# Head attention beside the main attention: 36 blocks one by one in place of 32 by twos, and experts that add into the output

## The reference, cut to what matters

```python
xn = layernorm(x)                                # x: 4 x 2048 x 256, float32
x  = x + attn(xn) + ffn(xn)

# attn: per token, the 16 heads attend to one another
Q, K, V = (xn @ W + b for each).reshape(B, S, 16, 16); rope on Q, K
out = softmax(einsum('bsid,bsjd->bsij', Q, K) / 4) @ V

# ffn: causal latent attention over the sequence, then 8 experts
x2 = xn + mla(rmsnorm(xn, g1))
t  = rmsnorm(x2, g2); top 2 of 8 by t @ gate_w, softmax of the two
ffn = x2 + sum over the two of gate * (silu(t @ w1[e]) @ w2[e])
```

## Time and profile before

| | us |
|---|---|
| median of 3 runs | 2903.67 (2902.66 to 2905.32) |
| the profiled execution | 2890.86 |
| its span, first to last instruction | 2889.0 |
| projections, to the attention's first POOL instruction | 424 |
| attention | 1546 |
| routing | 256 |
| experts | 633 |
| copy to `out` | 30 |

### The profile page before, as it was taken

The page is one execution under the profiler, slowest core; times in us unless marked ns, Lnnn a source line. Parts: engine busy times, 40 slices in busy tenths (PEclk is TensorE's granted clock), DMA queues, the critical chain, the costliest instruction groups (busy, mean ns, idle before and its releaser), DMA issues. The chain is left out here.

```text
span 2889.0 us, 58374 instructions
## 1 busy us (share of the span) xinstructions
PE 2543.6 (88%) x21356; PEld 1302.9 (45%) x21356; DVE 2236.6 (77%) x3720; ACT 1606.6 (56%) x2421; POOL 2113.7 (73%) x1196
## 2 busy tenths in 40 slices
PE   7999878999999999999999999996673988988892
PEld 4544432333333333333333333224563877777782
DVE  5557858899889988998899989902563899889970
ACT  2322225677777777777777777684442544444441
POOL 4543339698889888988898889884675777778772
PEclk9999999999999999999999999997775999999996
DMA  5785552133233323332333232105865565566555
GB/s 179 228 251 196 170 183 60 49 80 93 53 85 87 93 53 85 87 93 53 84 87 93 54 85 77 44 19 161 263 213 172 116 126 124 122 127 131 126 91 145
DMA packets 235945, 334.91 MB, mean 116 GB/s; under 512 B 30024, under 2 KB 175272, under 8 KB 234920
## 3 DMA queue, kind: packets, MB, share of 16 engines
q1 hardware_dynamic: 208072, 287.54, 34.4%
q0 software_dynamic: 27360, 39.73, 8.0%
q10 hardware_dynamic: 256, 4.19, 0.4%
HBM read 246.96 MB, written 154.04 MB: 139 GB/s over the span
## 5 line engine op out<-in xcount | busy, mean ns | idle before, releaser
L1047 DVE TENSOR_REDUCE p_piece_max<-p_ring 128x1 f32<-128x512 f32 (+3 forms) x2160 | 1293.2, 654 | 136.8 <-PE p_ring L157 66.8
L1105 ACT ACTIVATE p_probs<-p_st 128x1024 f32<-128x1024 f32 (+3 forms) x1280 | 1078.8, 897 | 413.9 <-PE p_st L1168 215.7
L1168 PE MATMUL p_st<-unit_q,unit_k 64*128 64x512 bf16 (+3 forms) x3520 | 432.7, 348 | 39.5 <-ACT p_probs L1105 23.2
L1186 PE MATMUL p_pv<-p_probs,unit_vg 128*32 128x512 f32 (+3 forms) x3520 | 412.1, 543 | 0.0
L1855 POOL DMA_INDIRECT acc<-p_y,p_rows x142 | 223.3, 1573 | 142.7 <-issue 56.1
L170 PE MATMUL p_ring<-unit_k,unit_q 64*128 64x512 bf16 (+3 forms) x1600 | 271.4, 352 | 27.9 <-DVE p_piece_max L1047 25.4
L964 POOL TENSOR_TENSOR p_terms<-p_head_in 128x4096 f32<-128x4096 f32 x32 | 282.9, 8839 | 8.9 <-DMA p_head_in<-head_qkv 4.6
L985 POOL TENSOR_TENSOR p_terms<-p_head_p,p_head_in 128x4096 f32<-128x4096 f32 x32 | 283.3, 8853 | 3.6 <-ACT p_head_p L1112 3.6
L2020 PE MATMUL p_y_ps<-p_w,p_hid 128*128 128x256 f32 x1136 | 276.8, 400 | 0.0
L969 POOL TENSOR_TENSOR p_terms<-p_terms 128x2048 f32<-128x2048 f32 (+2 forms) x96 | 252.7, 2632 | 17.4 <-POOL p_terms L969 11.4
L991 POOL TENSOR_TENSOR p_terms<-p_terms 128x2048 f32<-128x2048 f32 (+2 forms) x96 | 252.6, 2631 | 17.1 <-POOL p_terms L991 11.4
(11 more groups left out here) (192 smaller groups left out, 3477.5 us busy)
## 6 DMA issues: line engine op xcount, KB each, us to landing
p_w<-ffn_w SPq DMA_DIRECT2D x142, 512.0 KB
qk_parts<-p_parts SPq DMA_DIRECT2D x64, 384.0 KB, 3.6
head_qkv<-p_heads SPq DMA_DIRECT2D x16, 1536.0 KB, 6.8
p_rows<-rows_by_expert SPq DMA_DIRECT2D x71, 258.0 KB, 3.5
unit_q<-qk_parts SPq DMA_DIRECT2D x132, 128.0 KB, 3.2
unit_k<-qk_parts SPq DMA_DIRECT2D x132, 128.0 KB, 3.6
v_padded<-p_vx SPq DMA_DIRECT2D x16, 1024.0 KB, 8.0
p_head_in<-head_qkv SPq DMA_DIRECT2D x32, 384.0 KB, 4.2
```

Of the source, the lines that this page charges most:

```text
L1047: nc.vector.tensor_reduce(piece_max[:, n % 2, h:h + heads, i, pc], ring_ps[g % RING][:, 0:heads * width].rearrange("p (h k) -> p h k", h=h ...
L1105: nc.scalar.activation(probs[:, 2 * turn_of(s, i) + u, :, 0:width], st_ps[u][:, :, 0:width], ACT.Exp).then_inc(probs_done, 1)
L1168: last = nc.tensor.matmul(st_ps[u][:, half, 0:width], k6[s][rows, PAIR * second + u, kt * P:(kt + 1) * P], q6[s][rows, PAIR * second + u, ...
L1186: last = nc.tensor.matmul(pv_ps[hh * VW:(hh + 1) * VW, skip:CT], vg[s][:, kt, hh * VW:(hh + 1) * VW], probs[:, 2 * turn_of(s, i) + hh % PA ...
```

## The change

Three things are done. First, the attention stage takes 36 head blocks, the experts' stage 28. The blocks of the attention stage no longer go by twos within a unit but one by one: block m is weighed at about step 18 + 17.3 m of the 640 steps, whatever unit that is in. POOL runs weigh, shift of the next, score of the one after it. The exponentials' sums come first in weighing, and DVE inverts them (`reciprocal`) in place of POOL's `pow`. Three input slots replace two, POOL's loop is written out, and its waits no longer also increment the semaphore `apart`. Second, the routing stores `res` straight into `out`, the experts' stage adds to `out`, blank rows are dropped by a bounds check in the indirect DMA, and the last stage copies nothing. Third, blocks are added by fours with one DMA over two stretches of DRAM, 512 KB: the four early blocks at tile 1, the others at tiles 15, 24, 34, 43, 52, 61 and 70 (`ADDED`).

```diff
+MORE_BLOCKS = 4
+P2_BLOCKS = HEAD_BLOCKS + MORE_BLOCKS
...
+def early_block(m):
+    return block_of(m, 0) if m < HEAD_BLOCKS else block_of(m - MORE_BLOCKS, 1)
...
-        head_in = sb("p2_head_in", [P, 2, 3, H, DH])
+        head_in = sb("p2_head_in", [P, 3, 3, H, DH])
...
-        HEADS_AT = (12, 14)
         INVERSE_AT = 10
-        HEADS_STORED_AT = (12, 20)
+        weighed_at = lambda m: 18 + 173 * m // 10
+        MAXIMA_AT = {11 if m == 0 else weighed_at(m) - 14: m for m in range(P2_BLOCKS + 1)}
+        PROBS_AT = {weighed_at(m) - (1 if m == 0 else 4): m for m in range(P2_BLOCKS)}
+        HEADS_STORED_AT = {weighed_at(m) + 10: m for m in range(P2_BLOCKS)}
...
+        DIVIDED_AFTER = {max(m for m in range(P2_BLOCKS) if weighed_at(m) < N_STEP * (n + 2) - 8): n for n in range(UNITS - 1)}
...
-            def load_heads(m, u):
-                wait_apart(sp, head_done, m + 1, apart)
-                sp.dma_start(head_in[:, u, :, :, :].rearrange("p i h d -> p (i h d)"), head_qkv[block_of(m, 0)]).then_inc(head_loaded[u], 16)
-
-            def store_heads(m, u):
-                wait_apart(sp, head_done, 2 + m + 1, apart)
-                sp.dma_start(attn_rows[block_of(m, 0)], head_o[:, u, :, :].rearrange("p h d -> p (h d)")).then_inc(head_stored[u], 16)
+            def load_heads(m):
+                if m >= 3:
+                    sp.wait_ge(head_done, 2 + m - 2)
+                sp.dma_start(head_in[:, m % 3, :, :, :].rearrange("p i h d -> p (i h d)"), head_qkv[early_block(m)]
+                             ).then_inc(head_loaded[m % 3], 16)
+
+            def store_heads(m):
+                sp.wait_ge(head_done, 2 + m + 1)
+                sp.dma_start(attn_rows[early_block(m)], head_o[:, m % 2, :, :].rearrange("p h d -> p (h d)")
+                             ).then_inc(head_stored[m % 2], 16)
...
-                    if i in HEADS_STORED_AT:
-                        u = HEADS_STORED_AT.index(i)
-                        store_heads(2 * n + u, u)
-                        if n + 1 < UNITS:
-                            load_heads(2 * n + 2 + u, u)
+                    if N_STEP * n + i in HEADS_STORED_AT:
+                        m = HEADS_STORED_AT[N_STEP * n + i]
+                        store_heads(m)
+                        if m + 3 < P2_BLOCKS:
+                            load_heads(m + 3)
...
+            def weigh_heads(m):
+                u = m % 2
+                pool.wait_ge(head_probs_done, m + 1)
+                if m:
+                    pool.wait_ge(head_inverted, m)
+                src = head_p[:, u, :, :]
+                for width in (8, 4, 2):
+                    step(nc.gpsimd.tensor_tensor(head_sum[:, :, 0:width], src[:, :, 0:width], src[:, :, width:2 * width], ALU.add))
+                    src = head_sum[:, :, :]
+                nc.gpsimd.tensor_tensor(head_sum[:, :, 0:1], src[:, :, 0:1], src[:, :, 1:2], ALU.add).then_inc(head_summed, 1)
                 step(nc.gpsimd.tensor_tensor(
                     terms[:, :, :, :], head_p[:, u, :, :].unsqueeze(2).to_broadcast([P, H, DH, H]),
+                    head_in[:, m % 3, 2, :, :].unsqueeze(1).to_broadcast([P, H, DH, H]), ALU.mult))
+                for width in (8, 4, 2):
                     step(nc.gpsimd.tensor_tensor(terms[:, :, :, 0:width], terms[:, :, :, 0:width],
+                                                 terms[:, :, :, width:2 * width], ALU.add))
+                if m >= 2:
+                    pool.wait_ge(head_stored[u], 16 * (m // 2))
+                step(nc.gpsimd.tensor_tensor(head_o[:, u, :, :], terms[:, :, :, 0], terms[:, :, :, 1], ALU.add))
+                pool.wait_ge(head_inverted, m + 1)
...
-                step(nc.gpsimd.tensor_tensor(head_inv[:, :], head_sum[:, :, 0], minus_one[:, :], ALU.pow), before + 9)
...
-            def body(n):
-                for u in range(2):
-                    shift_heads(2 * n + u, u)
-                for u in range(2):
-                    weigh_heads(2 * n + u, u, n, steps(2 * n + 2, 2 * n + u))
-                for u in range(2):
-                    score_heads(2 * n + 2 + u, u, n + 2, steps(2 * n + 2 + u, 2 * n + 2))
-
-            body(0)
-            with pool.Fori(1, UNITS - 1) as n:
-                body(n)
-                divide(n - 1)
-            for u in range(2):
-                shift_heads(2 * (UNITS - 1) + u, u)
-            for u in range(2):
-                weigh_heads(2 * (UNITS - 1) + u, u, UNITS - 1, steps(2 * UNITS, 2 * (UNITS - 1) + u))
-            divide(UNITS - 2)
+            for m in range(2):
+                score_heads(m)
+            shift_heads(0)
+            for m in range(P2_BLOCKS):
+                weigh_heads(m)
+                if m + 1 < P2_BLOCKS:
+                    shift_heads(m + 1)
+                if m + 2 < P2_BLOCKS:
+                    score_heads(m + 2)
+                if m in DIVIDED_AFTER:
+                    divide(DIVIDED_AFTER[m])
...
-            def head_maxima(m, u):
-
-                dve.wait_ge(head_scored, m + 1)
-                nc.vector.tensor_reduce(head_max[:, u, :], head_s[:, u, :, :], AX_X, ALU.max).then_inc(head_max_done, 1)
+            def head_maxima(m):
+
+                if m < P2_BLOCKS:
+                    dve.wait_ge(head_scored, m + 1)
+                    nc.vector.tensor_reduce(head_max[:, m % 2, :], head_s[:, m % 2, :, :], AX_X, ALU.max).then_inc(head_max_done, 1)
+                if m:
+                    dve.wait_ge(head_summed, m)
+                    if m >= 2:
+                        dve.wait_ge(head_done, 2 + m - 1)
+                    nc.vector.reciprocal(head_inv[:, :], head_sum[:, :, 0]).then_inc(head_inverted, 1)
...
-                    if i - 2 in HEADS_AT:
-                        u = HEADS_AT.index(i - 2)
-                        head_probs(2 * n + u, u)
+                    if N_STEP * n + i in PROBS_AT:
+                        head_probs(PROBS_AT[N_STEP * n + i])
...
-                sp.dma_start(acc_v[b, c], res[:, c % 2, :, :]).then_inc(res_stored[c % 2], 16)
+                sp.dma_start(out_v[b, c], res[:, c % 2, :, :]).then_inc(res_stored[c % 2], 16)
...
-            sp.dma_start(acc[T:, :].rearrange("(r p) d -> p r d", p=P), blank[:, :, 0:D]).then_inc(tail_stored, 16)
...
-    NB = T // P - HEAD_BLOCKS
+    NB = T // P - P2_BLOCKS
...
-    sorted_rows, acc, table_i = SHARED["sorted"], SHARED["acc"], SHARED["table"]
+    sorted_rows, table_i = SHARED["sorted"], SHARED["table"]
+    acc = out_v.rearrange("b c p t d -> (b c t p) d")
...
-    ADDED = {STARTS[2 * k + 4] + 2: k for k in range(NB // 2)}
+    ADDED = {STARTS[4 * k + 6] + 2: k for k in range(NB // 4)}
...
+    ADDED_FIRST = NB // 4
...
-                        compute_op=ALU.add).then_inc(y_added, 16)
-
-            def add_pair(k, tiles):
-                for u in range(2):
-                    pool.wait_ge(oh_stored[u], 16 * (k + 1))
+                        bounds_check=T - 1, oob_is_err=False, compute_op=ALU.add).then_inc(y_added, 16)
+
+            def add_four(k, tiles):
+                if k < ADDED_FIRST:
+                    for u in range(2):
+                        pool.wait_ge(oh_stored[u], 16 * 2 * (k + 1))
                 pool.wait_ge(y_added, 16 * RT * tiles)
-                n = block_of(2 * k, 1)
-                rows_of_pair = lambda a: a.rearrange("(r s) d -> r (s d)", s=8)
-                nc.gpsimd.dma_start(rows_of_pair(acc[n * P:(n + 2) * P, :]),
-                                    rows_of_pair(attn_rows[n:n + 2, :, :].rearrange("a p d -> (a p) d")),
-                                    accum_op=ALU.add, max_dma_last_dim=4 * 8 * D).then_inc(pair_added, 16)
-                pairs[0] += 1
+                n = block_of(4 * k, 0)
+                halves = lambda a: a.rearrange("(c h r s) d -> c h r (s d)", c=2, h=2, s=8)[:, 1, :, :]
+                nc.gpsimd.dma_start(halves(acc[n * P:(n + 8) * P, :]),
+                                    halves(attn_rows[n:n + 8, :, :].rearrange("a p d -> (a p) d")),
+                                    accum_op=ALU.add, max_dma_last_dim=4 * 8 * D).then_inc(four_added, 16)
+                fours[0] += 1
...
+                if n == 1:
+                    add_four(ADDED_FIRST, n)
...
-    acc = SHARED["acc"][0:T, :].rearrange("(b c t p) d -> b c t p d", b=B, c=NC, p=P)
-    with SHARED["stack"], ExitStack() as ctx:
-        stored = [ctx.enter_context(nc.semaphore(f"p5_stored{i}")) for i in range(2)]
-        block = ctx.enter_context(nc.Block())
-        def store(eng, i):
-            for b in range(B):
-                for c in range(i * NC // 2, (i + 1) * NC // 2):
-                    eng.dma_start(out_v[b, c].rearrange("p t d -> t p d"), acc[b, c]).then_inc(stored[i], 16)
-            wait_apart(eng, stored[i], 16 * B * NC // 2, apart)
-        @block.sync
-        def _(sp):
-            store(sp, 0)
-        @block.scalar
-        def _(act):
-            store(act, 1)
+    route(*SHARED["route"], out_v)
```

(53 more changed lines are left out.)

58 lines of the change are left out of this document (23 added, 35 removed).

## The result

The changed kernel takes **2975.05 us** (median of 4, 2971.4 to 2976.73) against 2903.91 for the kernel before on the same chip (4 runs, 2902.66 to 2905.32): ratio 1.0243, 95% interval 1.0225 to 1.0261. It is slower by 71 us, where 84 us faster was forecast. The profiled execution took 2976.73 us (span 2975.0).

What follows compares the result with a forecast made beforehand. PE was taken to bound the attention, DVE close behind; in the experts PE, DVE and POOL had no slack for each other. Copy -32, experts -47, attention -4.5 sum to -83.5, from 2903.67 to 2820 us; range 2795 to 2915.

Steps and rivals of the forecast that it cites:

- The four add's transfer: Experts: 512 KB shared by all 16 engines takes 3.7 us for a pair's 1.8, putting POOL 6.9 us behind.
- Rival A: Experts: four adds run on two DMA engines, POOL becomes the chain, slower; 2930 us named, chance 0.25.
- PE's stretch: Experts: PE's run of 71 tiles with seven adds at 4.5 us each, 556.4 us against 605.1.
- SP passes the lag on: Experts: in SP's in-order queue, block loads wait for POOL's product and the next tile's rows stand behind them.
- It can win back 7.6 us from one add to the next: Experts, 28 blocks: POOL's work is 59.6 us against PE's 67.2, so it recovers 7.6 where it won 1.3.
- DVE needs 28 x 16.14 = 452 us for 64 x 7.35 = 470: Experts: DVE's work on 28 blocks fits on average, though two-tile blocks put it 1.4 us behind each time.
- The copy: Last stage: with experts adding into `out`, nothing follows the last indirect add, -32 us.
- rival B: Experts: the bounds check costs 0.6 us an indirect add; 2880 us (2867 to 2893), chance 0.09.
- The attention: Attention stage: +2.5 us for DVE's added work and -7 us for a stall that goes, together -4.5 us.
- The stall of the first unit: Attention, 460 to 470 us: DVE asks for block 1's maximum before POOL is done; its removal gives -7 us.
- Rival C: Attention: POOL can't keep the new rhythm and DVE, waiting, stops PE; +20, 2845 us, chance 0.06.
- Rival D: Experts: PE stalls little, 0 to 1 us per add; 2790 us, chance 0.08.

Runs made afterwards that it cites:

- e2: Changed kernel, four add still one DMA, its two dimensions exchanged so the slowest is the 32 rows, not the 2 stretches: 2827.19 us, ratio 0.9737.
- e9: e2 with all 8 four adds left out, their waits kept: 2784.96 us, ratio 0.959 to the kernel before.
- e13: e2 with SP issuing each head block's load behind the next tile's rows, not ahead: 2804.3 us beside 2881.34 for the kernel before, ratio 0.9729.
- e10: e2 with 32 head blocks in the attention and 32 in the experts, sums inverted on VectorE, 8 four adds: 2841.67 us, ratio 0.9794.
- e4: Kernel before with only the output in place of acc: experts and res write to it, bounds check, no copy at the end: 2875.59 us, ratio 0.9901.
- e1: Changed kernel with each four add issued as two DMAs of one stretch each: 2832.17 us, ratio 0.9746.
- e3: Kernel before with only its pair adds' pattern written as 2 stretches of 16 rows, same bytes and addresses: 2906.71 us, ratio 1.0005.
- e8: e2 with each of the attention's 36 reciprocals done twice on VectorE: 2830.97 us, ratio 0.9744.

## Why the prediction was wrong, step by step

- **The four add's transfer: the step that failed.** "Twice that is 3.7, so POOL falls 5.1 + 1.8 = 6.9 us behind" assumed that all 16 engines share the 64 packets. Two did. The landing is 24.1 us for a pair's 4.7, 19.4 more and not 1.8. With 16 engines it is 6.0, 1.3 more (e2). The two engines alone are 148 of the 155 us between forecast and result; the kernel that differs in nothing else (e2) takes 2827.19 against a forecast of 2820.
- **Rival A's mechanism is the one that acted, and its time was low.** Its second price for the packets was right: "the packets may run in two thirds of that" is 19.5 us on two engines, and the trace has 20.6. But with that price its sum gave 2881, and 2975 was measured. What was low is its chain: 71 x 3.03 + 56 x 3.99 = 439 us of POOL's work between the adds, where the experts take 518.2 without any add (e9), which is PE's rhythm. That the named 2930 lay half way is no merit of the sum. Rival A got a quarter of the chances because no direct copy of POOL's with a small outer size stood in the trace; the row of SP's queue was the right sign.
- **Four adds on 16 engines cost 5.4 us each,** 4.5 was forecast for the seven in PE's stretch. By the prediction's own measure PE's stretch is 564.2 us in e2 (2247.7 to 2811.9) for the forecast 556.4, of which the adds explain 6.3. Still, first to last add came out at 561.4, close to the forecast 605.7 - 47 = 559, and that was in part luck: the last indirect add starts 8.4 us behind PE's end, where it was 12.3 before and the forecast added 1.8.
- **The way it goes was half seen.** "SP passes the lag on" is what the waits show, but with that link loosened by a tile (e13) the experts won 3 us. It is one of several. "It can win back 7.6 us from one add to the next" did not help either: e2 has that room and pays 5.4 of a landing's 6.0 us. "DVE needs 28 x 16.14 = 452 us for 64 x 7.35 = 470" was true, and DVE's 65 us of waiting for POOL show that it does not bind with 28 blocks; with 32 it nearly does (e10).
- **The copy: -32, measured -29.7** (e4). The bounds check: 0, measured 0 (rival B is refuted: 1.566 us before and after).
- **The attention: -4.5 was forecast, and no gain is seen.** On one chip the last cast stands at 1872.5 and 1875.5 with the new attention (e2, e1) and at 1874.0 and 1874.4 with the old (e3, e4). The stall of the first unit did go: the first cast stands at 522.8 and 525.8 for 530.2 and 530.6, 4.4 to 7.8 us of the forecast 7, and PE is busy 9.60 us between 460 and 470 where it was 3.51. But the 14 units behind it take 1349.3 to 1351.1 us for 1343.5 to 1343.8, 5.5 to 7.6 more and not 2.5. The reciprocals explain little of it (e8: 0.9 to 2.7 for 7 us more of DVE), the 4 blocks 0.6 to 2.4 (e10); the rest goes with the order of the blocks or the places of the maxima and wasn't separated. Rival C's +20 is refuted; POOL was ahead of its loads and waited 54.8 us for them in 7 times.
- **Rival D** (0 to 1 us per add) is refuted by the 5.4.
- **The routing** is unchanged; the 13 us are a difference between executions.

## What to carry to other kernels

Before a DMA is made larger, look at the outermost dimension that its pattern has after the change: a rearrangement that gave one long dimension may leave a short one outermost when it skips rows, and 32 becomes 2. Writing the many-valued dimension first costs nothing and was worth 148 us here. And where in-order engines work in turn on the same items beside an engine without spare time, a delay of one of them reaches that engine by several links; loosening the link at which the wait is seen moved the wait to the next one here, without a gain, and only the delay itself (landing, number of adds) paid.

## What was not expected of the hardware

- A landing of 3.4 us plus 0.65 us per 8 KB accumulating packet of an engine, fitted to 4 and 32 packets (6.0 and 24.1 us), held within 0.5 us for 2, 8 and 16 (4.7, 8.3, 13.3).
- The issue of the same DMA on POOL is itself longer with few engines: 1.206 us for the four add on 2 engines, 0.969 with the dimensions exchanged; 1.081, 1.021 and 0.881 us for the pair on 2, 4 and 16.
- The start of the experts in the profiled executions lies between 2236.6 and 2267.9 us with the routing's code nearly unchanged (on more than one chip), more than most of the differences in question; only spans within a stage, or timed runs side by side, can be compared.
